# A two-layer graph network: rows picked by TensorE by node modulo 896, from a table in two float32r parts

## What is computed

```python
h = relu(layernorm(x))
agg = segment_sum(w[:, None] * (h @ W + b)[src], dst); deg = segment_sum(w, dst)
x = x + relu(agg / (deg + 1e-6))                                # layer 0
h = relu(layernorm(x))
m = gelu(concat([h[src], edge_attr]) @ W_msg + b_msg)
x = x + gelu(((1 + eps) * h + segment_sum(m, dst)) @ W_upd + b_upd)   # layer 1
```

## Time and profile before

| | |
|---|---|
| median of 3 runs | 3269.75 us (3269.13 to 3270.3) |
| span of the profiled execution | 3271.2 us |
| PE, PEld busy | 3160.8 us (97%), 3111.0 us (95%) |
| DVE busy | 2685.9 us (82%) |
| ACT busy | 1949.2 us (60%) |
| POOL busy | 2399.7 us (73%) |
| DMA | 286.46 MB, mean 88 GB/s |

### The profile page before, as it was taken

How to read it: one execution, slowest core, us unless ns; L and a number is a source line. 1 busy time by engine, 2 the same in 40 slices (tenths; PEclk the granted TensorE clock), 3 DMA queues, 4 the chain that set the end, 5 groups by cost and what they waited for, 6 DMA issues and landing times.

```text
span 3271.2 us, 104825 instructions
## 1 busy us (share of the span) xinstructions
PE 3160.8 (97%) x39149; PEld 3111.0 (95%) x39150; DVE 2685.9 (82%) x3320; ACT 1949.2 (60%) x6683; POOL 2399.7 (73%) x2539
## 2 busy tenths in 40 slices
PE   3999999999999999999889999999999999999999
PEld 3999999999999999999889999999999999999999
DVE  8888888888888887888688888888888888888885
ACT  5666666666666666666465555555555555555554
POOL 5777777777777777777467777777777777777775
PEclk9999999999999999999899999999999999999999
DMA  6333333333333333333233333344434443333342
GB/s 143 72 79 75 71 82 71 71 74 78 73 74 71 71 71 74 78 73 80 55 85 100 101 100 101 100 101 100 101 100 102 99 104 101 103 101 102 104 103 58
DMA packets 524716, 286.46 MB, mean 88 GB/s; under 512 B 283002, under 2 KB 458618, under 8 KB 524678
## 3 DMA queue, kind: packets, MB, share of 16 engines
q1 hardware_dynamic: 443910, 203.09, 23.2%
q0 software_dynamic: 80768, 82.87, 13.3%
HBM read 280.25 MB, written 5.50 MB: 87 GB/s over the span
## 4 chain that ended last, share of the span: by engine, by line
POOL 64%; issue 23%; PE 9%; DVE 2%; POOLq 1%; DMA 0%; ACT 0%; DVEq 0%; SPq 0%; ACTq 0%
POOL rows L499 64%; PE ps L762 4%; PE ps L769 2%; PE ps L798 1%; DVE pick_all L1100 1%; PE ps L866 1%; PE ps L791 0%; POOLq L495 0%; PE ps L826 0%; PE ps L896 0%; POOLq L510 0%; DMA rows<-h_table,idx 0%; DVE x_sb L1142 0%; POOLq L497 0%; DVEq L1158 0%
## 5 line engine op out<-in xcount | busy, mean ns | idle before, releaser
L1100 DVE TENSOR_SCALAR pick_all<-src_bc,node_f 128x2688 bf16<-128x2688 int16 x1372 | 2119.6, 1604 | 29.8 <-issue 28.9
L762 PE MATMUL ps<-parts,pick_all 128*128 128x192 bf16 x19208 | 1640.2, 246 | 24.7 <-DVE pick_all L1100 22.2
L762 PEld LDWEIGHTS ps<-parts,pick_all 128*128 128x128 bf16 x19208 | 1587.9, 98 | 36.2 <-issue 19.5
L499 POOL DMA_INDIRECT rows<-p_table,idx x1274 | 1202.6, 944 | 402.3 <-issue 402.3
L499 POOL DMA_INDIRECT rows<-h_table,idx x1250 | 1181.0, 945 | 390.8 <-issue 388.3
L769 PE MATMUL ps<-parts,pick_all 128*128 128x192 bf16 x9604 | 856.4, 246 | 5.5 <-issue 4.8
L769 PEld LDWEIGHTS ps<-parts,pick_all 128*128 128x128 bf16 x9604 | 797.2, 98 | 9.5 <-issue 8.4
L591 ACT ACTIVATE onehot<-iota,dw 128x72 f32<-128x72 f32 x1568 | 405.9, 342 | 0.0
L591 ACT ACTIVATE h_sb<-iota,dw 128x72 f32<-128x72 f32 x1568 | 405.9, 343 | 0.0
L1297 DVE TENSOR_TENSOR room<-ps,rows 128x512 f32<-128x512 f32 x196 | 135.5, 692 | 243.5 <-DMA rows<-p_table,idx 243.4
L523 ACT CAST idx<-src_tab 128x8 int32 (+1 forms) x392 | 78.1, 200 | 420.6 <-DMA rows<-h_table,idx 420.5
(11 more groups left out here) (108 smaller groups left out, 1706.3 us busy)
## 6 DMA issues: line engine op xcount, KB each, us to landing
src_bc<-last_src SPq DMA_DIRECT2D x196, 448.0 KB
ea<-in_edge_attr_dram SPq DMA_DIRECT2D x196, 256.0 KB
src_bc<-last_src SPq DMA_DIRECT2D x196, 224.0 KB
rows<-p_table,idx POOLq DMA_INDIRECT x1274
rows<-h_table,idx POOLq DMA_INDIRECT x1250
h_sb<-last_src SPq DMA_DIRECT2D x24, 224.0 KB
x_sb<-in_x_dram SPq DMA_DIRECT2D x12, 224.0 KB, 3.9
h_table<-h_sb SPq DMA_DIRECT2D x6, 224.0 KB
```

The costliest lines, as they stand in the source:

```text
L499: nc.gpsimd.indirect_dma_start(out=rows[:, s, j, 0:D], out_offset=None, in_=table[:, :], in_offset=bass.IndirectOffsetOnAxis(ap=idx[:, s, ...
L762: last = nc.tensor.matmul(psG[(s + shift) % 2], pick[layer][(s + shift) // 2 % 2][:, n, at:at + P], parts[:, n, :], start=(n == 0), stop=( ...
L1100: last = nc.vector.tensor_scalar(pick[layer][i][:, c * KB:(c + 1) * KB, :], src_bc[:, i, :, 0:w], node_f[:, c:c + 1], None, ALU.is_equal)
```

## The change

TensorE picks by residue and no longer by block. With span = 7 x 128 = 896, a node is 896 a + r, with r its residue and a from 0 to 6. The one-hot covers only the 896 residues (7 blocks k of 128). The table lies in SBUF so that for each block k the rows of all seven spans stand side by side: 7 x 64 = 448 columns. One picked tile is thus 7 blocks x 2 parts = 14 matmuls of 448 columns, which give for each edge the candidate rows of all seven spans. VectorE multiplies them by a mask over a (made once for all edges) and sums over a. The table is split in two parts of type float32r (high and remainder) and not in three of bfloat16. `picks_of` gives the tiles per group: NP = 2, 2, 2, 3 in layer 0 and 2, 2, 2, 2 in layer 1; GpSimd gathers the other 6, 6, 6, 5 and 6, 6, 6, 6. The extra and the `y` tiles go, `x_sb` keeps its values and isn't loaded again, and the key and mask work is added at the start.

```diff
+    NP = ((2, 2, 2, 3), (2, 2, 2, 2))
+    NPM = max(max(n) for n in NP)
+    BANKS = ((1, 4), (3, 5))
+    SPLIT = 2
-        parts = sb("parts", [P, NB, SPLIT * D], bf16)
+        parts = sb("parts", [P, SPLIT, KA, NA, D], f32r)
+        pick_all = sb("pick_all", [P, 2, KA * NPM * P], f32r)
+        mask = sb("mask", [P, NG, NPM, NA], bf16)
+        sel = sb("sel", [P, NPM, NA, D])
...
+            def load_bc(layer, b, q):
+                n, t = picks_of(layer, q)
+                v = keys.rearrange("k g e -> k (g e)")[:, bass.ds((b * SLOTS + q) * (NPM * P) + t * P, n * P)]
+                sp.dma_start(src_bc[:, q % 2, :, 0:n * P], v.rearrange("(a k) n -> a k n", a=1).to_broadcast(
+                    [P, KB, n * P])).then_inc(s_bc[layer][q % 2], 16)
+            def next_bc(layer, b, q):
+                sp.wait_ge(s_pick[layer], b * SLOTS + (q - 1))
+                load_bc(layer, b, q)
...
+            def picks(layer, b, q):
+                g = b * SLOTS + q
+                n, _ = picks_of(layer, q)
+                hot = pick_all[:, q % 2, 0:KA * n * P].rearrange("p (k e) -> p k e", k=KA)
+                pe.wait_ge(s_pick[layer], g + 1)
+                if q:
                     pe.wait_ge(s_prow[layer], g)
+                else:
+                    pe.wait_ge(s_parts[layer], UNITS)
+                for t in range(n):
+                    to = ps[:, BANKS[layer][q % 2] + t, 0:NA * D]
+                    for k in range(KA):
+                        for part in range(SPLIT):
+                            last = nc.tensor.matmul(to, hot[:, k, t * P:(t + 1) * P],
+                                                    parts[:, part, k, :, :].rearrange("p a d -> p (a d)"),
...
+            def highest(out, of):
+                meta(nc.vector.tensor_scalar(out, of, 7, None, ALU.logical_shift_right))
+                meta(nc.vector.tensor_scalar(out, out, 37, None, ALU.mult))
+                meta(nc.vector.tensor_scalar(out, out, 8, None, ALU.logical_shift_right))
+            dve.wait_ge(s_src, 64)
+            for half in range(2):
+                highest(calc[0:r, :, :], v)
+                nc.vector.scalar_tensor_tensor(out=key[0:r, half, :, :], in0=calc[0:r, :, :], scalar=-float(SPAN),
+                                               in1=v, op0=ALU.mult, op1=ALU.add).then_inc(s_key, 1)
...
+            def make_pick(layer, b, q):
+                n, _ = picks_of(layer, q)
+                dve.wait_ge(s_bc[layer][q % 2], (b * (SLOTS // 2) + (q // 2 + 1)) * 16)
+                nc.vector.tensor_scalar(pick_all[:, q % 2, 0:KA * n * P].rearrange("p (k e) -> p k e", k=KA),
+                                        src_bc[:, q % 2, :, 0:n * P], node_f[:, 0:1], None,
+                                        ALU.is_equal).then_inc(s_pick[layer], 1)
+            def next_pick(layer, b, q):
+                dve.wait_ge(s_picked[layer], b * SLOTS + (q - 1))
+                make_pick(layer, b, q)
+            def picked_rows(layer, b, q):
+                dve.wait_ge(s_picked[layer], g + 1)
+                dve.wait_ge(s_used[q % SLOTS], b + (layer * BODIES + q // SLOTS + 1))
+                dve.wait_ge(s_prow[layer], g + 1)
+                of = mask[:, bass.ds(g, 1), t:NPM, :].rearrange("p g t a -> p (g t) a")
+                nc.vector.tensor_tensor(sel[:, 0:n, :, :],
+                                        ps[:, bank:bank + n, 0:NA * D].rearrange("p t (a d) -> p t a d", d=D),
+                                        of.unsqueeze(3).to_broadcast([P, n, NA, D]), ALU.mult).then_inc(s_sel, 1)
+                dve.wait_ge(s_sel, b * SLOTS + (layer * NG + q + 1))
+                nc.vector.tensor_reduce(rows[:, q % SLOTS, J - n:J, 0:D],
+                                        sel[:, 0:n, :, :].rearrange("p t a d -> p t d a"),
                                         AX.X, ALU.add).then_inc(s_prow[layer], 1)
...
+            for q in range(2):
+                make_pick(0, 0, q)
+            dve.wait_ge(s_srct, 2)
+            meta(nc.vector.tensor_copy(high_i[:, :, :], src_tab[:, J0:J, :]))
+            highest(high_i[:, :, :], high_i[:, :, :])
+            meta(nc.vector.tensor_copy(high_f[:, :, :], high_i[:, :, :]))
+            nc.vector.tensor_tensor(mask[:, :, :, :].rearrange("p g t a -> p t g a"),
+                                    high_f[:, :, :].unsqueeze(3).to_broadcast([P, NPM, NG, NA]),
+                                    iota[:, 0:NA].unsqueeze(1).unsqueeze(1).to_broadcast([P, NPM, NG, NA]),
+                                    ALU.is_equal).then_inc(s_mask, 1)
```

More of the change, by code:

```diff
@@ L318, in _ @@
         def _(sp):
-            for one in (*s_used, *s_prow, s_yrow):
+            for one in (*s_used, *s_prow):
                 sp.sem_inc(one, 1)
@@ L576, in _ @@
             take(2, dst_tab, s_dwt)
-            for u in range(UNITS):
-                middle(0, u)
             take(4, w_tab, s_dwt)
@@ L679, in _ @@
             seed(UNITS - 2)
[L680 to L683 removed]
+            for u in range(4, UNITS):
+                high_of(u)
             seed(UNITS - 1)
@@ L748, in _ @@
                 turn(w_raw, half, psR[half])
-            def gather(layer, b, s, shift):
-                g = b * SLOTS + (s + shift)
-                pair = 2 * b + (s + shift) // 2
-                at = (s + shift) % 2 * P
-                pe.wait_ge(s_pick[layer], pair + 1)
-                if shift:
-                    pe.wait_ge(s_prow[layer], g)
-                for n in range(NB):
-                    if not shift and n % KB == 0:
-                        pe.wait_ge(s_parts[layer], n // KB + 1)
-                    last = nc.tensor.matmul(psG[(s + shift) % 2], pick[layer][(s + shift) // 2 % 2][:, n, at:at + P],
-                                            parts[:, n, :], start=(n == 0), stop=(n == NB - 1))
-                last.then_inc(s_picked[layer], 1)
@@ L766, in extra @@
-            def extra(layer, i, half):
-                for n in range(half * NB // 2, (half + 1) * NB // 2):
-                    last = nc.tensor.matmul(psX, pick[layer][i][:, n, PE2:PE3], parts[:, n, :],
-                                            start=(n == 0), stop=(n == NB - 1))
-                return last
-            def next_gathers(layer, b, s):
-                i = (s + 1) // 2 % 2
-                if s % 2:
-                    gather(layer, b, s, 1)
-                    if EXTRA[layer][i]:
-                        pe.wait_ge(s_xrow[layer], extras(layer, b + (s + 1) // SLOTS, i) - 1)
-                        extra(layer, i, 0)
-                else:
-                    if EXTRA[layer][i]:
-                        extra(layer, i, 1).then_inc(s_xpicked[layer], 1)
-                    gather(layer, b, s, 1)
@@ L924, in _ @@
             edge_transpose(0, 0, 0)
-            gather(1, 0, 0, 0)
-            if EXTRA[1][0]:
-                extra(1, 0, 0)
+            picks(1, 0, 0)
             edge_product(0, 0, 0)
```

370 lines of the change are left out of this document (107 added, 263 removed).

## The result

The changed kernel takes 3123.78 us (median of 4 runs, 3122.85 to 3126.58) against 3269.44 us before in the same session (3268.53 to 3270.3): a ratio of 0.9557, 95% interval 0.9543 to 0.957. The kernel is faster, by 145.7 us. The forecast was 2,993 us with a range up to 3,100, a gain of 276: the direction was right, the size was not, and the time lies above the range. Rival (a), TensorE passing GpSimd, is what happened.

What follows compares the result with a forecast made beforehand. GpSimd's gathers were taken to bound both loops, TensorE hidden just behind. Start and layer 0 1,442.6 + switch 59.95 + layer 1 1,467.2 + tail 25.05 = 2,994.8 us span; forecast 2,993, range 2,975 to 3,100.

Steps and rivals of the forecast that it cites:

- Rival (a): Both loops: TensorE becomes slower than GpSimd; 3,050 us at 200 ns per matmul, 3,110 at 205; chance 0.15.
- sum of 1,442.6: Start and layer 0: GpSimd resumes at 65.6 us, then 1,103 gather intervals of 1.2484 us, ending at 1,442.6.
- 448 columns take 186.7 + 2.5 = 189.2 ns: TensorE's picks: one float32r matmul of 448 columns comes every 189.2 ns, priced at the bf16 rate.
- The break-even: Both loops: above 195 ns per picking matmul, TensorE's body outlasts GpSimd's 28.7 us in layer 0 and 30.0 in layer 1.
- the tail: End of kernel, after the last gather start: expected to keep its 25.0 us.
- between the layers: GpSimd's wait at the switch from layer 0 to layer 1: expected to keep its 59.95 us, down to 55.
- upper bounds: VectorE's pick instructions at half rate with 4-byte output: 2.07 us, and 3.0 us for the three-tile group.
- The path from the three-tile group's picks to its windows: Layer 0: VectorE's product and reduction, then ScalarE's weighting; 5.4 us for the three-tile group, expected to be covered.
- above 4 us together: VectorE: product and reduction together taking over 4 us were named as a sign that would break the path to the windows.
- the cover of 6.3: TensorE's next picks (5.3 us) and one window (1.0) run before the window that needs the weighted rows: 6.3 us.
- Rival (b): TensorE's picks: 4-byte columns stream at half rate, 376 to 389 ns per matmul, about 5,200 us; chance 0.10.
- Rival (c): VectorE's half-rate picks and slow strided reads delay TensorE here and there; 3,100 to 3,260 us; chance 0.04.

Runs made afterwards that it cites:

- The kernel with one part: The changed kernel with the high part of the table alone, 7 matmuls per tile for 14: 3005.73 us, ratio 0.9191.
- The probe: The changed kernel with seven loops of extra float32r, bf16 and float32 matmuls behind its last update product, to time single matmuls: 3162.1 us in one run.

## Why the prediction missed

- **GpSimd: right.** 221 gathers fewer, a pace that neither VectorE nor 118 GB/s of transfers changes. The kernel with one part shows the sum of 1,442.6 as 1444.45. It was a floor, not the bound.
- **TensorE: the step that failed.** "448 columns take 186.7 + 2.5 = 189.2 ns" carried bf16's 2.5 ns to a type that no row showed, by the argument that the pass is then "of the bf16 kind". Measured are 202.7 ns settled and, with the 280 to 305 ns from a block's first pick to its second, 205.1 in layer 0; in layer 1 it is 208.1, as every fourth block also runs at 206.5. The reasoning on the rate was right (one pass, one column per cycle, not two), but the term beside it is 16 ns and not 2.5, and in the loops the pitch is 16 and 19 ns above the forecast's. The break-even stood in the text, 195 ns, 6 ns above the value taken; the 0.15 for rival (a), a price just beyond it, was too little for a value without a row of its own. With 126 and 112 matmuls per body, 1 ns is 11.7 us.
- **The size of rival (a).** By its own formula, (205.1 - 195) x 126 x 49 = 62 us and (208.1 - 195) x 112 x 49 = 72 us. Beside it stood a seam of 0.37 us per body in layer 0 and two windows of 2.00 to 2.04 where 4.1 for both was allowed (+15), and other products of layer 1 that take 7.5 us for the 8.1 allowed (-29). Measured: 30.24 - 28.7 = 1.5 us per body, 75 us, and 30.81 - 30.0 = 0.8, 40 us. In the table the first shows as +71.7, the second as +22.7 and the tail's +19.8: for the first 650 us of layer 1 GpSimd only gets ahead of TensorE, until its four slots are full, and this lead is what the tail still has to work off.
- **What the rival left out.** It priced the loops alone. Where the bound moves from the gatherer to the consumer, the backlog is paid at the next barrier: +14.1 us between the layers. With the measured prices the rival's formula gives 2,993 + 62 + 15 + 72 - 29 = 3,113 us, with those 14 us 3,127, against 3,123.8.
- **VectorE: covered, but by less than was written.** Picks came at their upper bounds (2075 and 3002 ns), products at 1088 and 1558 as forecast, reductions at 1750 and 2571, between the two values given (1.1 and 2.2; 1.55 and 3.1). The path from the three-tile group's picks to its windows is 6.5 us, not 5.4: the forecast's "above 4 us together" came true (4.1). It had been summed with the lower of the two values for the reduction; with the upper it would have been 1.55 + 3.1 + 2.03 = 6.7 us against the cover of 6.3. It costs nothing only because TensorE's slower picks fill it; with 13 matmuls a tile it costs 0.1 us per body over GpSimd's pace, and the backlog between the layers with it.
- **The rest.** The first pick starts at 52.0 (51.7 forecast), GpSimd resumes at 67.35 (65.6), no group waits for a load of sources. Rival (b) is refuted: no half rate, and no sum of weight load and columns. Rival (c)'s time of 3,100 to 3,260 would have held the result, but by another mechanism: VectorE waits for TensorE, not the other way round.

The Trainium skill ("SBUF — State Buffer", A bandwidth-pool intuition that's wrong (but worth ruling out)) gives TensorE's moving operand some 614 GB/s for bf16. The probe's float32r rows move 128 partitions x 448 x 4 bytes in 202.7 ns, 1,132 GB/s. So the figure can't be read as a limit for 4-byte columns, as rival (b) did; the measurement decides.

What stays open: where float32r's 13 to 16 ns come from (its weight load or its columns), and why it is 16 at 448 columns and 13.3 at 384 and 256; why a quarter of layer 1's blocks run at 206.5 ns a pick and the others at 202.7.

## What to carry to other kernels

Where the margin between two engines is 3% and a new type of instruction appears over a hundred times per body, no rate taken from another type is good enough: state the break-even first, and give the side beyond it the chance that an unmeasured term deserves. Relieving the bound engine by moving work to the next one stops paying at their crossing, and the best split is on the near side of it: one tile less on TensorE in layer 0 was worth 33 us, as the engine that is just late also pays its backlog at every barrier. A path that is just covered is found by adding to it: what comes through (1.45 us of the 1.56 added per body here) tells the cover.

## What the runs showed of the hardware

- A float32r matmul streams one 4-byte column per cycle at 2.4 GHz (256 columns in 120.0 ns, 384 in 173.3, 448 in 202.7), with 13 to 16 ns beside it; bf16 and one record of a full float32 matmul, at two cycles per column, have 2.5.
- VectorE's comparison from int16 runs at half the rate into float32r: 1,792 elements in 2075 ns, into bf16 in 1141. A reduction whose inner step is strided takes 1750 ns for 896 elements, where the product that makes the same 896 takes 1088.
- With a wait of 1.27 us on TensorE once per body of 32 us, the granted clock fell behind that wait in seven of 49 bodies, and the next 8 to 10 picks came 373 ns apart; with a wait of 0.23 us (thirteen matmuls) it didn't fall in layer 0's loop.
